# A four-layer audio tower on one core: the keys' and values' loads of an expert tile go from SyncE's queue to ScalarE's

## The reference, cut to what matters

```python
def _expert(x, Wqkv, bqkv, Wo, bo, g1, be1, W1, bf1, W2, bf2, g2, be2):
    qkv = x @ Wqkv.T + bqkv
    q, k, v = split into 8 heads of 16
    attn = softmax(einsum('bhqd,bhkd->bhqk', q * scale, k))
    ctx = (attn @ v) @ Wo.T + bo
    x = _layernorm(x + ctx, g1, be1)
    h = gelu(gelu(x @ W1.T + bf1) @ W2.T + bf2)
    return _layernorm(x + h, g2, be2)
gated = probs * mask_of_top_2          # every token has two experts
return einsum('ebsd,bse->bsd', every expert's output, gated)
```

## Time and profile before

| | us |
|---|---|
| median of 3 runs | 3249.82 (3234.05 to 3255.95) |
| the profiled execution | 3245.33 |
| its span in the profile | 3243.5 |
| PE busy in the span | 2765.3 |
| ACT busy | 1882.0 |
| DVE busy | 1840.4 |
| POOL busy | 546.3 |

### The profile page before, as it was taken

One profiled execution on the slowest core, in us unless ns is written; L12 is line 12 of the kernel. 1 busy time (PEld: TensorE's weight loads), 2 busy tenths in 40 slices (PEclk: granted clock), 3 DMA queues, 4 the chain that ended last, 5 costly groups with the idle time before them and its releaser, 6 DMA issues.

```text
span 3243.5 us, 66796 instructions
## 1 busy us (share of the span) xinstructions
PE 2765.3 (85%) x24695; PEld 1942.8 (60%) x24695; DVE 1840.4 (57%) x4886; ACT 1882.0 (58%) x4218; POOL 546.3 (17%) x728
## 2 busy tenths in 40 slices
PE   7788785899998999899988977688888888888898
PEld 5456454566766666666666653465565656556676
DVE  4664666567666677666676732344544444454454
ACT  2232233577776777677676768377348644754343
POOL 2000003234234433433222130000000000000000
PEclk9886887899999999999999988799899989999998
DMA  5000005766566776675565520100000000000000
GB/s 209 1 10 30 1 6 196 235 203 197 181 182 195 214 220 191 193 223 180 171 175 160 154 99 6 44 1 1 14 11 1 1 14 5 1 1 14 6 1 6
DMA packets 162466, 304.09 MB, mean 94 GB/s; under 512 B 19729, under 2 KB 121226, under 8 KB 154442
## 3 DMA queue, kind: packets, MB, share of 16 engines
q1 hardware_dynamic: 158818, 293.69, 29.4%
q0 software_dynamic: 3328, 6.14, 0.6%
HBM read 227.00 MB, written 72.75 MB: 92 GB/s over the span
## 4 chain that ended last, share of the span: by engine, by line
PE 50%; DVE 15%; issue 11%; ACT 10%; DMA 4%; DVEq 4%; POOL 3%; POOLq 1%; PEld 1%; ACTq 1%; PEldq 0%; SPq 0%
PE ps L1870 4%; PE ps L1535 4%; PE ps L1553 4%; PE ps L1514 4%; DMA xg<-slots_x 4%; PE ps L1348 3%; PE ps L1940 2%; PE ps L2002 2%; PE ps L1578 2%; PE ps L1802 2%; PE ps L1587 2%; PE ps L1964 2%; ACT hid L2332 2%; PE ps L1333 2%; DVE peaks L2697 1%
## 5 line engine op out<-in xcount | busy, mean ns | idle before, releaser
L2697 DVE TENSOR_REDUCE peaks<-ps 128x1 f32<-128x748 f32 x608 | 557.1, 932 | 270.1 <-PE ps L1514 252.4
L2185 ACT ACTIVATE pt<-ps 128x384 f32<-128x384 f32 x1216 | 562.2, 491 | 193.7 <-PE ps L1535 178.1
L1535 PE MATMUL ps<-qst,kst 98*128 98x128 bf16 x3648 | 392.5, 224 | 14.9 <-ACT pt L2185 9.7
L1535 PEld LDWEIGHTS ps<-qst,kst 98*128 98x128 bf16 x3648 | 244.9, 99 | 171.0 <-ACT pt L2185 56.6
L1166 POOL TENSOR_TENSOR rstd<-var,minus_half 128x6 f32<-128x6 f32 x40 | 52.9, 1323 | 1668.1 <-DVE var L2602 1218.7
L1514 PE MATMUL ps<-kst,qst 96*128 96x374 bf16 x1216 | 305.6, 333 | 12.7 <-DMA kst<-saved_k 5.5
L1553 PE MATMUL ps<-pt,vst 128*32 128x128 f32 (+1 forms) x7296 | 273.1, 282 | 0.0
L1553 PEld LDWEIGHTS ps<-pt,vst 128*32 128x32 f32 (+1 forms) x7296 | 188.8, 112 | 89.6 <-issue 59.5
L1514 PEld LDWEIGHTS ps<-kst,qst 96*128 96x128 bf16 x1216 | 100.1, 100 | 26.1 <-DVE qst L2775 6.7
L2775 DVE CAST qst<-ps 96x1024 bf16<-96x1024 f32 x76 | 92.6, 1219 | 37.0 <-PE ps L1465 36.3
L1964 PE MATMUL ps<-xnT,QT 128*128 128x374 f32 (+5 forms) x256 | 94.4, 473 | 6.4 <-ACT shared L2382 5.1
(11 more groups left out here) (659 smaller groups left out, 6528.8 us busy)
## 6 DMA issues: line engine op xcount, KB each, us to landing
kst<-saved_k SPq DMA_DIRECT2D x76, 1176.0 KB
wf<-in_l SPq DMA_DIRECT2D x76, 512.0 KB
vst<-saved_v SPq DMA_DIRECT2D x76, 408.0 KB, 3.3
saved_k<-kparts SPq DMA_DIRECT2D x144, 192.0 KB, 3.9
saved_v<-vprod SPq DMA_DIRECT2D x32, 408.0 KB, 3.6
rows<-in_l_rows SPq DMA_DIRECT2D x76, 128.0 KB
saved_k<-kst SPq DMA_DIRECT2D x48, 192.0 KB, 2.7
slots_x<-zeros SPq DMA_DIRECT2D x4, 1216.0 KB, 11.4
```

Source lines behind the costliest of these rows:

```text
L1535: mm = pe.matmul(out[:, c * P:(c + 1) * P], kst[0:STACK + SHIFT, m % 3, head, j * P:(j + 1) * P], qst[0:STACK + SHIFT, m % 3, head, :], st ...
L2185: act.activation(pt[:, u % (2 * GROUP), :], entry()[:, 0:H0], ACT.Exp, scale=float(HD) ** -0.5)\
L2697: v.tensor_reduce(peaks[:, g, head:head + 1], entry()[:, :, 0:T // 2], XY, ALU.max)\
```

## The change

`load_k` and `load_v` leave SP's program and go into ACT's, at the same places of the list. ACT reads the tile's expert number itself with a `value_load` of its own, once per tile (in `load_k`; `load_v` uses the register again). All waits stay in form: `ring_done` and `lifted` are semaphores that ACT itself counts up. SP keeps its own `value_load`s and all other loads and stores.

```diff
--- before.py
+++ after.py
-                def load_k(m):
...
-                    e = owner_of(m)
-                    sp.dma_start(kst[0:STACK + SHIFT, m % 3, :, :].rearrange("p e t -> p (e t)"), of_owner(saved_k[b], e))\
-                        .then_inc(S[f"k_loaded{m % 3}"], 16)
-
-                def load_v(m):
...
+                def of_owner(table, m):
+                    if m not in owners:
+                        owners[m] = act.value_load(owner[0:1, m:m + 1], min_val=0, max_val=E - 1)
+                    return table[bass.ds(owners[m], 1), :, :].rearrange("o p n -> (o p) n")
+
+                def load_k(m):
+                    b = m // TILES
+                    if m == 0:
+                        act.wait_ge(S["rows_filled"], 32)
+                    if m % TILES == 0:
+                        for i in range(2):
+                            act.wait_ge(S[f"k_saved{i}"], 96 * E // 2 * (b + 1))
+                            act.wait_ge(S[f"v_saved{i}"], 16 * E // 2 * (b + 1))
+                    if m >= 3:
+                        act.wait_ge(S["ring_done"], scored[m - 3])
+                    act.dma_start(kst[0:STACK + SHIFT, m % 3, :, :].rearrange("p e t -> p (e t)"), of_owner(saved_k[b], m))\
+                        .then_inc(S[f"k_loaded{m % 3}"], 16)
+
+                def load_v(m):
+                    if m >= 2:
+                        act.wait_ge(S["lifted"], 2 * (m - 2) + 2)
+                    act.dma_start(vst[:, m % 2, 0:V_USED], of_owner(saved_v[m // TILES], m))\
+                        .then_inc(S[f"v_loaded{m % 2}"], 16)
+
                 for what, *at in expert_steps():
+                    n.take("ring_done", ENTRIES.get(what, 0))
                     if what == "scores":
                         scores(*at)
+                        scored[at[0]] = n.now("ring_done")
+                    elif what == "load_k":
+                        load_k(*at)
+                    elif what == "load_v":
+                        load_v(*at)
+                        owners.pop(at[0])
```

More of the change, by code:

```diff
@@ L1062, in experts @@
                         load_wq(*at)
[L1063 to L1066, removed]
                     elif what == "load_att":
@@ L2198, in up @@
                     last.then_inc(S["ring_done"], 1)
+                owners, scored = {}, {}
+                def of_owner(table, m):
[19 more added lines that the diff above has]
+                        .then_inc(S[f"v_loaded{m % 2}"], 16)
                 for what, *at in expert_steps():
+                    n.take("ring_done", ENTRIES.get(what, 0))
                     if what == "scores":
                         scores(*at)
+                        scored[at[0]] = n.now("ring_done")
[4 more added lines that the diff above has]
+                        owners.pop(at[0])
                     elif what == "shift":
```

## The result

| | kernel before | changed kernel |
|---|---|---|
| median | 3246.42 us (18 runs, 3234.05 to 3256.37) | 3266.18 us (18 runs, 3254.94 to 3275.49) |
| ratio to before, 95% interval | | 1.0061, 1.0048 to 1.0074 |
| span of the profiled execution | 3243.5 us | 3266.3 us |

The changed kernel is 0.6% slower, about 20 us. The forecast was 3247, which is 3 us less than the 3249.8 it started from; 3266 lies inside the range of 3220 to 3290, but the change went the other way.

The account below looks back on a forecast made before the run. PE was taken to set the expert phase's pace. From the profiled 3245.3 us, minus 13 for the gain, plus 9 on ACT, plus 1 for the opening gives 3242.3, a median of 3247; range 3220 to 3290.

Parts of the forecast that it names:

- What bounds the kernel: Expert phase: PE sets the pace, busy 1193.9 of 1305 us, while ACT has about 328 us free.
- The gain: PE's waits for xg in the expert phase: 17 of at most 26 us come back, less 4, so 13 us.
- x1n took 4 us of it back: In the 11 turns where PE stood for xg, x1n becomes late next, at 0.4 us a turn.
- rival C: Transfers on shared engines: xg comes no sooner, or kst itself comes late; +10 us gives 3260; chance 0.17.
- 17.9 + 8 us: All xg can give: PE's 17.9 us of waits in 11 turns plus 8 us for fallen clock after three stalls.
- The cost on ACT: Keys' and values' loads bring ACT 1.31 us a tile, 100 us in all, mostly hidden; 9 us taken, bounds 0 and 100.
- mark for trouble: Signs of a wrong forecast: PE waits for pt, kparts or x1T of 40 us or more; ACT TENSOR_LOAD well above 0.45 us.
- ACT's sequencer can do part of it: On ACT, moved work partly runs under the score tile before it, about 0.5 us, which would halve the 13 us price.
- The opening: First batch: ACT waits for the saved keys ahead of the first query copy; 1 us taken, bounds 0 and 4.
- B: ACT becomes the bound at the keys' and values' places in every turn; price 100 us, half gives 3288; chance 0.18.
- D: All goes well: xg's 26 us come back and ACT's work is hidden, giving 3224 us; chance 0.15.

Follow-up runs that it names:

- e3: Changed kernel without ACT's lookup of the expert number, every tile loading expert 0's keys and values: 3247.93 us, ratio 1.0017 to the kernel before.
- e6: Changed kernel with ACT's lookup of the next tile's expert number moved to the turn before, at step 13: 3250.84 us, ratio 1.0010 to the kernel before.
- e9: Changed kernel with every tile's expert number read twice in a row on ACT: 3334.52 us, ratio 1.0285 to the kernel before.

## Why the prediction was wrong, by its own steps

**What bounds the kernel.** Right: PE sets the pace, and the rows of the wait views named what would change.

**The gain.** This is the first step that failed. The wait went as expected: xg's from 17.9 to 3.5 us. That x1n took 4 us of it back is not clear: read to 1925 us in all four, its wait is 38.9 and 40.0 in the two executions of before and 42.0 and 41.2 in the two of the changed kernel. What failed is the step from a shorter wait to a shorter time: of "Gain: 13 us" some 5 us are seen in the xg turns, and the bias rows and the other heavy turns took as much or more. The prediction had the premise in its own rival C ("in the bad turns SP's backlog of weights, their rows and saves is larger than that"), but sought the late transfer in kst and vst or in xg itself, not in what stood in the backlog with xg and had no queue of its own. It also took one profile's 17.9 + 8 us as a fixed stock, when the same turns give back 7.8 us by themselves from one execution of before to the next.

The rule of the Trainium skill ("DMA: Bandwidth & Descriptors", section "Queues, rings and completion order") that an engine takes turns between queues fits the fall of xg's waits and wq's landing of 4.2 instead of 2.8 us, though no view here shows the packets' order. xg itself landed in 6.0 us in the early-lookup kernel, the only one with the keys on ACT for which the view has a landing: sooner than 7.5, and not the 3 to 5 of the prediction. The sentence that several issuing engines save only the issue time (the Trainium skill, "Trainium Kernel Development and Optimization", section "Key Constraints") does not fit the waits, which did move from one transfer to another; read as a sentence on the sum of the work it fits e3 and e6, where two queues bring no time.

**The cost on ACT.** This is the second step that failed, in its size: 9 us in the sum, some 20 us measured (19.2 and 21.8 in the keys turns, against 1.3 in the second execution of before). With the gain at nothing, it alone gives the sign. Three parts of it were off.
- The place. I read the keys' load in a turn without keys (0.1 us exposed, 52 turns) and the values' issue in a turn with keys (0.33 us exposed, 24 turns), and gave each kind one of them. The chip did the reverse: the quiet turns lose nothing clear (-1.0 and +1.4 over 18), since x1n itself is late there (0.66 us), the lookup is short, and the hole lies under that wait; in the keys turns the values' issue is nearly hidden (in the turn shown PE is 0.18 us behind up to the score tile ahead of the query), and the hole ahead of x1T adds 0.63. Together that is 0.81 in this turn; the measured sum, 19.2, is 0.80 in each of the 24. The view of waits shows only half of it (9.4 us in 20 waits for x1T), since PE's standing is split between short pieces; the prediction's mark for trouble, waits of 40 us, would have missed it. The turns had to be measured. The waits for pt did not grow (9.5 us).
- "ACT's sequencer can do part of it while the score tile before it is still running (about 0.5 us)." True, of the lookup as of the issue: 0.50 us of the lookup ran under the score tile in the keys turn shown. It did not halve the price, because the whole was not 0.98 us.
- The size. In the keys turn shown it is 1.75 us from the lookup's start to the end of the issue, so 1.25 stand beyond the score tile and not 0.48. The lookup is 458 ns in the median as expected (452), but 745 there; the keys' issue is 577 ns there where SP had 373. The prediction's own mark for trouble, a TENSOR_LOAD on ACT well above 0.45 us, is met in the turns that count and hidden in the median.

**The opening.** Right: 1 us was taken. The first query copy, expected after 575.6, came at 575.15, and from the bias product of the first query to PE's first product with the keys it took 11.74 us instead of 11.06, so 0.7.

**The rivals.** B (ACT becomes the bound) was right in its mechanism and set its point wrongly: it needed 0.6 us a tile over 76 tiles, and 0.8 in 24 was enough to turn the sign. Its price of half or all of 100 us didn't come, but e9 shows how near it was: a second lookup of 0.46 us a tile in the median (1.06 us in the keys turns) cost 70 us, a part of it in the clock. C forecast 3260, nearest to the result, by way of a cost on ACT of 9; its "xg stays late" did not happen, and of its new waits for kst there is one of 1.8 us. D fell with the gain.

What the sum should have been: 0 (gain and loss in the queues) + 19.2 + 0.7 = 19.9 us more, which from the median of 3246.4 gives 3266.3, and the changed kernel's is 3266.2. The 0 is not measured by itself: it is what e3 and e6 leave room for (0.17% and 0.10%, with no change inside both intervals).

## What to carry to other kernels

Before a load moves to a busy engine, read that engine around the very place in every kind of turn. Add up all that the load brings (the read of a number, its registers, the issue) and set it against the one instruction that runs beside it: only that much is hidden. What can be done elsewhere, like the read, goes a turn earlier, where the engine waits anyway. Take the duration of a piece from the turns that count, since a median over all turns can hide them. A wait for the last transfer of a full queue is not stock to be claimed: sum what the queue must carry there, and ask which other transfer becomes the last. Where turns repeat to a few hundredths in one group and wander by several in another, price the first from one profile and the second only from several.

## What was not expected of the hardware

- A register load on ACT took 448 to 1207 ns. 75 of the 76 began beside a running activation, so that is not what makes one long: 47 ended under it. The long ones stand at the end of the keys turns (median 0.73 us, others 0.45). A second one right behind it (e9) took 286 in the median, but 827 in the same kind of turn. In 22 of the 24 cases in which SP was issuing the saves of the keys at that moment the load took over 520 ns, and in 2 of the 52 others; but in e6, at its other place, 23 that met such saves took 447 to 462. So the cause stays open. SP's own median for the same operation fell from 452 to 268 ns once the keys' issue was gone from its queue; that wasn't followed up.
- The issue of one and the same load, the keys, took 567 ns on ACT and 373 on SP.
- A wait of PE of 1.50 us was followed by 4 us at a granted clock of 0.53, one of 0.44 us at the same place by a clock of 1.00. The waits between do not sort cleanly: in e9 one of 1.40 us was followed by 1.00 and another of 1.40 by 0.54, and in the changed kernel's second execution one of 0.66 by 0.74.
